# Two of four turned state tiles scaled by ScalarE in the last six units of a half-turn, with other stations and shorter rings

## The reference

```
h = layernorm(x) * (1 + scale) + shift ; h = h[perm]       # 512 rows of each sequence
xm, z = split(h @ W_in)                                     # 2 x 1024 channels
xm = silu(causal_conv(xm, 4 taps))
dtr, B, C = split(xm @ W_xp)                                # 64, 16, 16
dt = softplus(dtr @ W_dt + b_dt)
for each state s of 16:   hst[s] = scan(hst[s] * exp(dt * A[s]) + dt * xm * B[s])   # along time
y = sum over s of hst[s] * C[s]  + xm * D
out = x + gate * ((y * silu(z)) @ W_out)[inv_perm]
```

## Time and profile before

| | us |
|---|---|
| time before, median of 3 (3078.62 to 3079.0) | 3078.77 |
| the profiled execution: its own time | 3080.79 |
| the profiled execution: span of its instructions | 3078.7 |
| layer 1, first scan to last scan | 1083.2 to 3021.7 |
| turn 3, first scan to first scan of turn 4 | 1808.6 to 2054.5 |
| busy in the span: PE, VectorE, ScalarE, GpSimd | 2696.0, 2371.9, 1602.6, 1872.3 |

### The profile page before, as it was taken

The page is one execution under the profiler, slowest core; times in us unless marked ns, Lnnn a source line. Parts: engine busy times, 40 slices in busy tenths (PEclk is TensorE's granted clock), DMA queues, the critical chain, the costliest instruction groups (busy, mean ns, idle before and its releaser), DMA issues. The chain is left out here.

```text
span 3078.7 us, 32722 instructions
## 1 busy us (share of the span) xinstructions
PE 2696.0 (88%) x11066; PEld 1510.2 (49%) x11066; DVE 2371.9 (77%) x3068; ACT 1602.6 (52%) x2414; POOL 1872.3 (61%) x821
## 2 busy tenths in 40 slices
PE   7999999999999766988988988898898897897964
PEld 3556466466465344554454454455455454444542
DVE  3455455455454389999999989999998998999993
ACT  1222223223222476775775776676676687577550
POOL 0112111211213097888899799799799789889891
PEclk9999999999999978989999989999998999998976
DMA  6012022212214344455574665565566466556653
GB/s 211 7 54 76 28 103 89 89 55 89 89 55 151 119 99 96 109 118 125 134 163 113 148 154 120 135 160 123 133 157 140 120 152 141 123 138 141 158 130 73
DMA packets 261596, 355.29 MB, mean 115 GB/s; under 512 B 21597, under 2 KB 115937, under 8 KB 261434
## 3 DMA queue, kind: packets, MB, share of 16 engines
q1 hardware_dynamic: 202200, 246.46, 25.9%
q0 software_dynamic: 55680, 105.93, 19.9%
q10 hardware_dynamic: 3554, 0.88, 0.1%
HBM read 215.56 MB, written 71.58 MB: 93 GB/s over the span
## 5 line engine op out<-in xcount | busy, mean ns | idle before, releaser
L1943 POOL TENSOR_TENSOR hs<-slots,b_wide 128x2048 f32<-128x2048 f32 x256 | 1258.8, 4942 | 242.6 <-PE bank L1486 166.5
L2106 DVE TENSOR_TENSOR_SCAN hs<-bank,hs 128x512 f32<-128x512 f32 x1024 | 1220.9, 1210 | 30.1 <-ACT bank L1731 20.4
L1731 ACT ACTIVATE bank<-dt,decay 128x512 f32<-128x512 f32 x1024 | 701.5, 693 | 543.4 <-DVE hs L2106 541.5
L1486 PE MATMUL bank<-ident,hs 128*128 128x128 f32 x4096 | 671.2, 291 | 282.7 <-DVE acc L2124 232.1
L1486 PEld LDWEIGHTS bank<-ident,hs 128*128 128x128 f32 x4096 | 499.5, 148 | 818.3 <-DVE acc L2124 308.9
L2124 DVE SCALAR_TENSOR_TENSOR acc<-bank,c_t,acc 128x512 f32<-128x512 f32 x772 | 562.7, 729 | 62.8 <-PE bank L1486 58.6
L1438 PE MATMUL bank<-h_t,w_in 128*128 128x512 f32 x1024 | 505.8, 600 | 1.0 <-ACT h_t L1651 1.0
L1985 POOL DMA_DIRECT2D acc<-scaled x252 | 276.5, 1097 | 43.8 <-DMA acc<-scaled 32.5
L1534 PE MATMUL bank<-w_y,zs 128*128 128x512 f32 x512 | 253.4, 601 | 1.3 <-DVE zs L2223 1.3
L1449 PE MATMUL bank<-w_out,h_in 128*128 128x512 f32 x448 | 230.3, 640 | 1.5 <-ACT dt L1698 1.3
L776 PE MATMUL bank<-z_t,w_k 128*128 128x512 f32 x512 | 221.2, 592 | 0.9 <-ACT z_t L875 0.9
(11 more groups left out here) (163 smaller groups left out, 3116.6 us busy)
## 6 DMA issues: line engine op xcount, KB each, us to landing
b_wide<-b_rows SPq DMA_DIRECT2D x256, 256.0 KB, 3.7
acc<-scaled POOLq DMA_DIRECT2D x252, 256.0 KB, 5.0
w_in<-in_L_cond_W_in SPq DMA_DIRECT2D x128, 256.0 KB, 4.2
z<-in_x SPq DMA_DIRECT2D x8, 2048.0 KB, 9.5
res<-in_x SPq DMA_DIRECT2D x8, 2048.0 KB, 9.7
h_tiles<-h_t SPq DMA_DIRECT2D x56, 256.0 KB, 2.8
h_in<-h_tiles SPq DMA_DIRECT2D x56, 256.0 KB, 4.7
x_rows<-w_part POOLq DMA_DIRECT2D x28, 512.0 KB, 8.2
```

The source lines that it names most:

```text
L1486: last = nc.tensor.transpose(bank[:, j * P:(j + 1) * P], hs[:, slot, j, t * P:(t + 1) * P], ident[:, :])
L1731: nc.scalar.activation(decay_banks[N % 3][:, :], dt[:, H % 2, j, :], ACT.Exp, scale=g.decay[:, 4 * (H % 2) + j, s:s + 1]).then_inc(da_read ...
L1943: nc.gpsimd.tensor_tensor(hs[:, U % RING, :, :], slots[:, H % SLOTS, :, :], b_wide[:, U % B_RING, :].unsqueeze(1).to_broadcast([P, 4, CHUNK]),
L2106: nc.vector.tensor_tensor_scan(block, decay_banks[N % 3][:, :], block, 0.0, ALU.mult, ALU.add).then_inc(scanned, 1)
```

## The change

From unit 10 of each half-turn on (six units), ScalarE scales tiles 1 and 3 and VectorE adds 0 and 2. Both scaled tiles go in one accumulating transfer, of 512 KB. The last half-turn of the program keeps three tiles. The buffer `scaled` is twice as large; the rings of `w_in` and `b_wide` have three slots (two in the branch for long permutations, which does not run with these inputs). Nearly all stations are set anew. The core of the diff:

```diff
-W_IN_RING = 4
-B_RING = 4
+W_IN_RING = 3
+W_IN_RING_ON = 2
+B_RING = 3
+B_RING_ON = 2
-THREE_TILES = 16
+THREE_TILES = 10
+LAST_HALF = BATCH * UNITS - STATE
...
-ADD_W_AT = (7, 30, 32, 37)
+ADD_W_AT = (8, 31, 33, 38)
...
     if U >= DIRECT:
-        return CT
-    return 3 if U % STATE < THREE_TILES else 2
+        return tuple(range(CT))
+    return (0, 1, 2) if U % STATE < THREE_TILES or U >= LAST_HALF else (0, 2)
+
+def scaled_of(U):
+    return tuple(t for t in range(CT) if t not in tiles_of(U))
...
-        scaled = sb("scaled", [P, SCALED_RING, 1, 512])
+        scaled = sb("scaled", [P, SCALED_RING, 2, 512])
...
-                    if 0 <= U < DIRECT and n % 4 >= tiles_of(U):
+                    if 0 <= U < DIRECT and n % 4 in scaled_of(U):
                         scale_state(U, n % 4)
...
-                n = tiles_of(U)
-                if U % STATE == THREE_TILES and U % STATE > 0:
+                if U % STATE == THREE_TILES:
                     need(pool, summed, sums_before(U))
-                nc.gpsimd.dma_start(acc[:, U // STATE % 2, n:, :], scaled[:, U % SCALED_RING, 0:CT - n, :], accum_op=ALU.add).then_inc(state_pooled, DMA)
+                n = len(scaled_of(U))
+                sums = acc[:, U // STATE % 2, 3:, :] if n == 1 else acc[:, U // STATE % 2, 1::2, :]
+                nc.gpsimd.dma_start(sums, scaled[:, U % SCALED_RING, 0:n, :], accum_op=ALU.add).then_inc(state_pooled, DMA)
...
-                return (step - lag,) if U >= 0 and 0 <= step - lag < tiles_of(U) else ()
+                return (step - lag,) if U >= 0 and step - lag in tiles_of(U) else ()
```

More of the change, by code:

```diff
@@ L1215, in load_w_y, with load_w_in @@
                 sp.dma_start(w_y[:, :, :], a["L1_cond_W_out"].rearrange("(k p) n -> p k n", p=P)).then_inc(w_y_loaded, DMA)
-            def load_w_in(stage, m, before):
+            def load_w_in(stage, m, slot, before):
                 if before is not None:
@@ L1221, in load_w_in @@
                 at = m if stage == "xm" else KI + m
-                sp.dma_start(w_in[:, m % W_IN_RING, :, :], w_in_dram[:, :, at * P:(at + 1) * P]).then_inc(w_in_loaded[m % W_IN_RING], DMA)
+                sp.dma_start(w_in[:, slot, :, :], w_in_dram[:, :, at * P:(at + 1) * P]).then_inc(w_in_loaded[slot], DMA)
             def load_next_w_in(b, stage, m):
@@ L1230, in load_next_w_in @@
                     before = filled_by(PLACES[b0], stage0, m0)
-                load_w_in(stage, m, before)
+                load_w_in(stage, m, w % W_IN_RING, before)
             def store_b(place):
@@ L1426, in norm_turned, with project_in @@
                 last.then_inc(fills(place, "h", i), 1)
-            def project_in(place, stage, m, ks, loads):
+            def project_in(place, stage, m, ks, slot, loads):
                 if ks[0] == 0:
                     out = claimed(pe, place, stage, m)
-                    need(pe, w_in_loaded[m % W_IN_RING], DMA * (loads + 1))
+                    need(pe, w_in_loaded[slot], DMA * (loads + 1))
                     if stage == "xm" and m == 0:
@@ L1437, in project_in @@
                 for k in ks:
-                    last = nc.tensor.matmul(work_bank(place, stage, m)[:, :], w_in[:, m % W_IN_RING, k, :], h_t[:, place.par, k, :],
+                    last = nc.tensor.matmul(work_bank(place, stage, m)[:, :], w_in[:, slot, k, :], h_t[:, place.par, k, :],
                                             start=(k == 0), stop=(k == KD - 1))
@@ L1616, in body @@
                         place = chunk_place(b, c)
[L1617 removed]
+                        loads = 2 * KI // W_IN_RING_ON * it
                         for i in range(KD):
@@ L1620, in body @@
                         for m in range(KI):
-                            project_in(place, "xm", m, range(KD), loads + m // W_IN_RING)
+                            project_in(place, "xm", m, range(KD), m % W_IN_RING_ON, loads + m // W_IN_RING_ON)
                         project_xd(place, range(KI))
@@ L1631, in body @@
                         for m in range(KI):
-                            project_in(place, "z", m, range(KD), loads + KI // W_IN_RING + m // W_IN_RING)
+                            project_in(place, "z", m, range(KD), m % W_IN_RING_ON, loads + KI // W_IN_RING_ON + m // W_IN_RING_ON)
                         for j in range(KI):
@@ L2142, in add_states @@
                 else:
-                    need(dve, summed, sums_before(U - 1) + min(t, tiles_of(U - 1) - 1) + 1)
+                    need(dve, summed, sums_before(U - 1) + sum(i <= t for i in tiles_of(U - 1)))
                 if U >= DIRECT and t >= 2:
```

92 lines of the change are left out of this document (47 added, 45 removed).

## The result

| | us |
|---|---|
| time after, median of 5 (3089.2 to 3094.83) | 3091.09 |
| time before on the same chip, median of 5 (3078.04 to 3079.34) | 3078.77 |
| ratio | 1.0041 [1.0029, 1.0053] |
| the profiled execution after: its own time, its span | 3090.36, 3088.5 |

The change makes the kernel 12.3 us slower. The forecast was 3077, no change; 3091 lies inside its range and 14 us above its value.

What follows compares the result with a forecast made beforehand. VectorE bounds layer 1, except at the seam of two turns, where GpSimd's path is equally long. -30.7 + 4.2 + 25.5 - 0.5 = -1.5 us against the profiled 3080.8 gives 3079.3; runs lie 2.0 lower: 3077, range 3044 to 3104.

Steps and rivals of the forecast that it cites:

- part 5: Rings and stations: shorter rings and moved stations cost nothing, with 5 us to either side.
- part 4: Seam of two turns: double transfers lengthen GpSimd's path, 4.25 us lost in each of six seams, 25.5; the seventh gains 0.5.
- part 1: VectorE: six additions fewer per half-turn save 3.84 us; the eight first half-turns keep 30.7 us.
- Part 2: ScalarE: 90 more scalings hidden on the whole; two `silu_x` cost 0.6 us in each of seven turns, 4.2 us.
- Part 3: Double transfer in the first half-turn: costs nothing, since GpSimd waits for its full ring there anyway.
- slower, by ScalarE or PE: Rival: tile 1 needs an older transfer landed, ScalarE's wait holds up decays; 3092 us, chance 0.08.

Runs made afterwards that it cites:

- e11_addw: e1_single with the additions of `w_part` and the `fin` loads and stores back at their old units: 3081.56 us, ratio to before 1.0012.
- e1_single: The changed kernel with three tiles added by VectorE in every unit, so new stations and rings alone: 3066.31 us, ratio to before 0.9959.
- e2_first: The changed kernel with two scaled tiles only in units 10 to 15 of all turns, not in 26 to 31: 3060.91 us, ratio 0.994.
- e6_bytes: The changed kernel, but the accumulating transfer carries tile 3 alone (256 KB); tile 1 is scaled and never added: 3056.45 us, ratio 0.9926.
- h1_ring: The changed kernel without the load of `gate`, with a fourth slot for scaled tile 1: 3098.38 us; without that slot 3094.53.
- e9_silu: e8_first7 with the first two `silu_x` of a turn at blocks 43 and 68 instead of 45 and 63: 3059.4 us, ratio to before 0.9936.
- e8_first7: e2_first without the last turn, so two scaled tiles only in units 10 to 15 of turns 0 to 6: 3060.55 us, ratio to before 0.9939.
- e3_second: The changed kernel with two scaled tiles only in units 26 to 31: 3098.2 us, ratio to before 1.0065.

## Why the prediction was wrong

Each term of its sum beside what the runs give for it (differences of medians, so each only to a few us):

| term | forecast | measured | from |
|---|---|---|---|
| part 5 and other stations | 0 | +2.8 | e11_addw less before |
| additions of `w_part` a unit later, with the `fin` tables (inside part 4, 2.25 a seam) | -13.5 | -15.3 | e1_single less e11_addw |
| first half-turns (parts 1, 2, 3) | -26.5 | -5.4 | e2_first less e1_single |
| seam without `w_part` (the rest of part 4) | +38.5 | +30.2 | after less e2_first |
| sum | -1.5 | +12.3 | |

**Part 4 and its seams: right in the mechanism.** A doubled landing takes 1.2 to 1.8 us more at five of its six places, forecast 1.5; the seam was GpSimd's; VectorE's release in the second half-turns is lost behind it whole, as e6_bytes shows. GpSimd's waits for landings are 59.3 us, forecast 60, those of VectorE for GpSimd 29.8, forecast over 25, and from unit 28 to unit 8 it is 2.9 us longer on the average of the first six seams (2.2 shorter at the first, then 2.5 to 6.3 longer), forecast some 4. The longer issue before the gather costs 0.48 where 0.6 was taken: from the issue to the gather of `y_rows` it is 2.52 us (1822.67 to 1825.19), in e6_bytes 2.04 (1812.29 to 1814.33). What the text had not seen is ScalarE's part in it, its wait of 4.25 us for a slot in unit 1; h1_ring shows that this is a second path of the same length and not a cost of its own. The sum for the seams was 8.3 too high. The landings that it priced in full, of the transfers of units 30, 0 and 3, are longer by 1.8, 1.2 and 1.3, little less than its 4.5. But against e1_single the first seam pays only 1.5 us from unit 28 to unit 8, the next five 5.2 to 8.1, where 6.5 a seam was forecast; why the first is cheap was not looked into. (The text says five waits and lists six; the sum has the right ones.)

The Trainium skill (DMA: Bandwidth & Descriptors, section Anatomy of one DMA, SWDGE path) would have priced 256 KB more at an estimated 0.6 us. The trace does not agree: 1.2 to 1.8 us at five places, above it by two to three times.

**The additions of `w_part`: about right in size, and easily missed.** The prediction folded them into part 4 as a cancelled landing and 0.75 us, 13.5 in all. By the stretches of the profiled executions units 27 to 8 give 10.7 of it. With the `fin` tables, whose share is not known, they are the largest single gain of the change, and it could be had without the doubling.

**The step that failed is the size of parts 1 to 3, by 21 us.** The mechanism of part 1 was right, 3.84 us for six additions: turn 7 shows it undisturbed in units 11 to 16. But the sum let nearly all of it stand, and two costs were mis-sized.
- *Part 2*, ScalarE's two `silu_x`, taken at 0.6 us a turn with an upper bound of 2.6. Turns 0 to 6 gain 2.0 us each in units 11 to 16 (e1_single to e2_first, 313.6 to 299.3) in place of 3.84, and lose 1.0 in units 17 to 26 (529.1 to 536.1): 2.8 a turn on the average, 19.6 in seven, where 4.2 stood. (It is 3.2 in each of turns 1 to 6, where unit 17 grows from 9.4 to 10.6 and units 18 to 26 stay as they were, and 0.7 in turn 0.) The idle rows of turn 3 add to 2.85. The prediction counted only a decay that comes late. There are three ways for the delay: the decay (0.48 and 0.50), the first tap of the convolution (0.69), and the state bank that PE waits for, with its projections behind it (0.90 and 0.28). The 1.67 of decays and tap are ScalarE's by the order of its rows. The 1.18 at unit 17 are not its alone: PE is full there, 0.82 of waiting for it is left in e9_silu where ScalarE does not hold it, and the prediction had no term for PE. How these 1.18 divide is open, and so is whether VectorE would have kept the gain with ScalarE out of the way.
- *Part 3*, taken at nothing, is right in turns 0 to 6, by all that the rows show, and not in turn 7. The full ring at 1936.01 was of turn 3. With the change units 11 to 16 take 7.1 us on average in turns 1 to 6 (42.7 in all) and 6.0 in turn 7 (35.8); the 512 KB of e2_first land in 6.0 us in the median, and half a microsecond goes by before the next issue. So in turn 7 GpSimd's chain becomes the bound in the first half-turn too, and up to 7.1 us are lost (4.5 with e8_first7 as the base).

**The rivals.** The case that happened is mostly the last, "slower, by ScalarE or PE", 3092, with a chance of 0.08: it had both upper bounds of part 2, 18 us, where 19.6 were measured (by its terms its time would be 3091). It named PE too, without a price. That the total fits so well is partly luck, since part 3's 7.1 and the 8.3 too many of part 4 nearly cancel. Part 2 called ScalarE's work hidden on the whole because it waits over 500 us in all; that total says nothing of the few places where it does 3.7 us of work in one piece.

## What to carry to other kernels

When work is moved from the bound engine to one with much idle time, look at the longest uninterrupted piece in that engine's order, not at the sum of its waits: a piece that just fits into a unit of the bound engine may not fit once the unit is 10% shorter, and it holds up every consumer at once, here scans, taps and the transposing PE. Look also for units in which a third engine is already as long as the bound one, here PE with 9.4 of 9.4 us in unit 17: what is taken off the bound engine there or just before is not gained. Where transfers follow each other in a chain (each waits until the one before has landed), the landing plus the half microsecond seen here is the least length of a unit, so more bytes in each transfer lengthen the units that were near it; compare the two before pairing tiles. And take the parts of such a change apart: here a small reordering of transfers was worth some 15 us, three times what the doubling brings where it is best, and the whole hid both.

## What the runs showed of the hardware

- An accumulating transfer within SBUF grows with its bytes by much less than in proportion: 42 transfers of 512 KB in e3_second land in 7.0 us in the median, the 210 of 256 KB of the same kernel in 5.1; at the same place it is 1.2 to 1.8 us more (five places) or nothing (one).
- From such a landing to the issue that waited for it there are 0.54 us in the median of the 28 waits of e3_second.
- The accumulation's issue holds GpSimd longer for twice the bytes: the next tensor operation starts 0.77 us behind the issue at 1807.83, and 0.60 behind the one at 1798.87 in e6_bytes.
- The tensor operations `hs` of GpSimd take 5.07 us in the mean in place of 4.94; whether that is the queue's traffic or the neighbours' was not tried.
